# A kernel of four chained attention layers: new places for all steps in the orders of its five engines

## The reference

```
x = L0(ctx, x)    # attention over the context, 4-wide GELU, self attention of the norm, skip
x = L1(x, ctx)    # linear attention with elu, norm
x = L2(x, ctx)    # 16 heads of self attention, 16 heads over ctx, 8 experts (top 2), residuals
x = L3(x, ctx)    # 16 causal heads, norm, 16 heads over ctx, norm, ffn of 512 with relu, norm
```

```
scores = einsum('bhqd,bhkd->bhqk', q, k) / sqrt(dh)
attn   = softmax(scores);  out = einsum('bhqk,bhkd->bhqd', attn, v)
h1 = gelu(einsum('nd,efd->enf', hf, fc1_w) + fc1_b)
eo = einsum('enf,edf->end', h1, fc2_w) + fc2_b
```

## Time and profile before

| | |
|---|---|
| three runs | 2834.36 us median (2832.34 to 2839.7) |
| the profiled execution | 2836.33 us, of which the span from first to last instruction is 2834.1 |
| granted clock of TensorE, mean | 0.913 |
| PE busy | 2400.3 us, 85%, 27712 matmuls |
| PEld | 1672.2 us, 59% |
| DVE | 1536.4 us, 54% |
| ACT | 1521.5 us, 54% |
| POOL | 544.8 us, 19% |
| DMA queue of SP | 79.91 MB, 11.5% of 16 engines' span |

### The profile page before, as it was taken

How to read it: one execution, slowest core, us unless ns; L and a number is a source line. 1 busy time by engine, 2 the same in 40 slices (tenths; PEclk the granted TensorE clock), 3 DMA queues, 4 the chain that set the end, 5 groups by cost and what they waited for, 6 DMA issues and landing times. The chain is left out here.

```text
span 2834.1 us, 69952 instructions
## 1 busy us (share of the span) xinstructions
PE 2400.3 (85%) x27712; PEld 1672.2 (59%) x27712; DVE 1536.4 (54%) x4449; ACT 1521.5 (54%) x2379; POOL 544.8 (19%) x730
## 2 busy tenths in 40 slices
PE   3656989898989989898989889897989989888975
PEld 2434647575666657575666657574756657564643
DVE  3343555656465565656465665656465565634232
ACT  1324545565665555665656655665555565644432
POOL 2111112121212222121212121121212122111111
PEclk9555989999999999999999999999999999998965
DMA  2100010111010110101010101111010111110000
...
DMA packets 103752, 84.21 MB, mean 30 GB/s; under 512 B 15000, under 2 KB 102681, under 8 KB 102937
## 3 DMA queue, kind: packets, MB, share of 16 engines
q1 hardware_dynamic: 103449, 79.91, 11.5%
...
...
## 5 line engine op out<-in xcount | busy, mean ns | idle before, releaser
L984 DVE TENSOR_REDUCE smax<-by_query_banks 128x8 f32<-128x616 f32 (+1 forms) x512 | 515.9, 1008 | 353.6 <-PE by_query_banks L1303 353.1
L770 ACT ACTIVATE probs<-by_key_banks 77x1024 f32<-77x1024 f32 (+1 forms) x512 | 517.8, 1011 | 216.7 <-PE by_key_banks L1325 213.3
L1240 PEld LDWEIGHTS by_key_banks<-moe_w,hid 128*128 128x128 f32 x4096 | 476.0, 192 | 14.1
L1240 PE MATMUL by_key_banks<-moe_w,hid 128*128 128x128 f32 x4096 | 483.7, 275 | 0.0
L752 ACT ACTIVATE hid<-by_query_banks,cols 128x512 f32<-128x512 f32 x512 | 334.9, 686 | 274.0 <-PE by_query_banks L1231 272.0
L1373 PE MATMUL weighed_bank<-probs,values 128*32 128x128 f32 x8192 | 365.3, 301 | 2.2 <-ACT probs L770 1.6
L1303 PE MATMUL by_query_banks<-k_int,q_int 32*128 32x128 f16 (+1 forms) x4096 | 199.9, 220 | 166.5 <-DVE smax L984 87.3
L1303 PEld LDWEIGHTS by_query_banks<-k_int,q_int 32*128 32x128 f16 x4096 | 121.7, 99 | 334.0 <-issue 220.1
L1373 PEld LDWEIGHTS weighed_bank<-probs,values 128*32 128x32 f32 x8192 | 211.0, 117 | 95.3 <-issue 45.7
L1325 PE MATMUL by_key_banks<-q_int,k_int 32*128 32x128 f16 x4096 | 223.2, 233 | 8.1 <-ACT probs L770 5.3
L765 ACT ACTIVATE m_sb<-turned_bank 16x128 f16<-16x128 f32 x256 | 67.7, 264 | 298.1 <-PE turned_bank L1355 298.1
(11 more groups left out here) (232 smaller groups left out, 3878.5 us busy)
## 6 DMA issues: line engine op xcount, KB each, us to landing
q_int<-q_nat SPq DMA_DIRECT2D x256, 128.0 KB, 2.7
k_int<-k_nat SPq DMA_DIRECT2D x128, 128.0 KB, 2.7
k_int<-k_nat SPq DMA_DIRECT2D x128, 77.0 KB, 2.3
...
q_int<-m_sb SPq DMA_DIRECT2D x256, 4.0 KB
...
```

Of the source, the lines that this page charges most:

```text
L770: act.activation(probs[h % 2][0:nk], by_key[0:nk], ACT.Exp, scale=DH ** -0.5)\
L984: dve.tensor_reduce(smax[h // 2 % 2][:, pair, :], scores, AX.X, ALU.max, negate=True)\
L1240: last = pe.matmul(B[e % 2][:, seq_tok(b)], hidden[e % 2][:, c, seq_tok(b)], moe_w2[:, e, c, :], start=(c == 0), stop=(c == CHUNKS - 1))
```

## The change

The five strings of TURNS are replaced by others of the same length with the same number of each letter. The length is 232 letters, one for each step of HEAVY, LIGHT, LAYERS and INPUTS. Nothing else differs: the instructions of each step, the streams' own orders, the buffers and the semaphores stay. The first line for PE:

```diff
 TURNS = {
-    "PE": "iiiiiihxlhhxxxllhlhllhhllhxlhlhllhhxhhlhhllxhhhlhlhhllhhlllhhhhxxxhhhhhhxhxhxhhhhhhxhhhhhhhhhhxh"
+    "PE": "ihxlhhxhlxlhllhllhlhxxlhlhlhhhllhxhlhlxhhlhihlhhlhlhlhhlhihxxhhlihhhhxxhxhhhxhhihhxhhhhhhhhhhhxh"
...
 }
```

More of the change, by code:

```diff
@@ L127 @@
-    "SP": "iiiiiillllllxxxxxhhhhhhhhhhhhhhhhhhhhhhhhhhhhhhhhhhhhllllllllllllllllxxxxxxhhhxhhhhhhhhhhhxxxhhh"
-          "hhhhhhhhhhhhhhhhhhhhhhhhhhhhhxxxxxxxxxxxxxxxxxxxhhhhhhhhhhhhhhhhhhhhhhhhhhhhhhhhhhhhhhhhhhhhhhhh"
-          "hhhhhhhhhhhhhhhhhhhhhhhhhhhhhhhxxxxxxxxx",
+    "PE": "ihxlhhxhlxlhllhllhlhxxlhlhlhhhllhxhlhlxhhlhihlhhlhlhlhhlhihxxhhlihhhhxxhxhhhxhhihhxhhhhhhhhhhhxh"
+          "hhhhhihxhhhhhhhhhxhhhhhhhxhhhhhhhhhhxhhhhxhhxhhhhhxhhhhhhhhxhhhhhhhhxhhhhhhhhxxhhhhxhxxhhhhhhhhh"
+          "xhhhhhhxhhhhxxxxhxhxhhhhxxhhhhxhhxxhhhxh",
@@ new lines @@
+    "ACT": "hxhhlhllhlhxlllhixhilllxhlhhxhhxhihlllhlhhxhlhhlhlhihhhhhxxllhxihhhhhlhxxhhhhhxihhxhhhhhhhlhhhhh"
+          "xhhhhhhxhhhhhhhhhhhhxhhhhhxhhhhhhhhhhhxxxxhhhhhhhhhhhhhhhhhhhhhhxhhhhhxhhhxhhxhxhhhhhhhhhxhxhhhh"
+          "hhxhhhhhxhxhhxxxhxhxhxxhhhhhhhxhhxhhxhhx",
+    "DVE": "lhxlxxhlhlllhxhlhhllllhhxlhihhhlxhhhlhlhlllxhhllhhllhhhhxxhhxhhhihhhhhhxhhhxhxhhhhhhhhhhhhhhhxhx"
+          "hhhxhhhhhhhhhhxhhhxhhhhhhhhhhhhhhhhhhxxhhxhhhhhhhhxhhhhhhhhhhxhhhxhhhhhhxhhhxhxhhhxhhhhxhhhhhhhx"
+          "hhhhhhhxhhxhxxxhxxhxihxhihhhhihhxxxhxhih",
@@ new lines @@
+    "POOL": "xhlllhxhhhhhhlllhhhhhhhhhhlllhhlhhhhhhhhhhhhhhhhhhhhhhhhhhhhhhhhhhhhhhhhhhhhhhhhhhhhhhhhhhhhhhhh"
+          "hhhhhhhhhhhhhhhhhhhhhhhhhhhhhhhhhhhhhhhhhhhhhhhxlhhlhllxhlllllhlhxhhllxxxxxxxxxxhxxxxxhxxxhhxhxh"
+          "hixhxxihhihhhxhxihxxxxxixhxhhxxhxxhxxihh",
+    "SP": "hhhihxxlhhxihlhlhhhihlhhlihihlhixhhhhxhhhhhlxhlhhlllhhhhhxhhxxhlhxhhhxhhxhhhhhhlhhlllxhhlxhhhhhh"
+          "xxhhhhhhlhhxhxhhhhhhllhhhxxhhxxhhhhhhlxhhhhhhhhhhhxhhxxhlhhxhhhhhhhhhhhhhhxhxxhxhhhhhxhhhhhxhxhh"
+          "hhhhhhhhhhhhhhhhhxhxhhxhxxhhxhhxhxhhhxhh",
```

## The result

The changed kernel takes 2946.4 us (median of 4 runs, 2934.2 to 2961.5), the kernel before 2833.4 us (2826.2 to 2839.7) beside it: a ratio of 1.0405, 95% interval 1.0378 to 1.0432. That is 113 us slower; the forecast was 100.

The account below looks back on a forecast made before the run. It took PE, busy 85% of the span in a tight chain with reductions and exponentials, as the bound. Terms summed to 7.3 us a pass, 95 over thirteen passes, plus 5 outside: 2934 us, 3.5% slower; 80% range 2874 to 2980.

Parts of the forecast that it names:

- A: SELF2's seven copies, issued later, hold ACT at proj2, and DVE's proj2 half delays a reduction; 3.2 us a pass.
- B: SELF3's copies: max3_2's copy goes behind query2's seven, so PE waits for it in score0_1; 1.7 us a pass.
- C: Norm n32 on DVE now precedes back0_0, so max2_1 on PE waits for o_norm; 0.8 us a pass, router included.
- D: End of the pass: PE reaches caq_turn before hat is complete; 1.6 us of waiting, 0.45 us a pass kept.
- E: Experts: in3_1 waits for gelus, x1_elu stands later, l1_hat delays out4_1 and out6_0; 0.75 us a pass.
- F: The gain: query0 on PE fills the wait between score1_3 and score1_4, -0.1 us a pass; other listed moves are free.
- G: The clock: waits of 3 us can bring one more stretch at 1.2 GHz; 0.5 us a pass.
- second rival: New PE waits among the heads lower the clock more: 3.8 us instead of 0.5, 10.6 a pass, 2980 us; 14%.
- Faster: query0 in PE's gap at the heads' start keeps the clock up, giving back up to 3.8 us a pass; 2821 us; 5%.

Follow-up runs that it names:

- x1: The kernel before with only two SyncE copy steps moved, max1_1 ahead of proj0 and max1_3 ahead of query0; 2884.9 us.
- x2: The kernel before with only two SyncE copy steps moved, proj2 ahead of max3_1 and query2 ahead of max3_2; 2873.5 us.
- x5: x4 with the end-of-pass order of TensorE and ScalarE (caq_turn and the steps around it) as in the kernel before; 2845.8 us.
- x6: x4 with VectorE's n32_norm put ahead of score2_3 again, as in the kernel before; 2851.2 us.
- x7: x4 with the returns of x5 and x6 both made in one kernel; 2856.9 us.
- x4: The changed kernel with SyncE's order of the kernel before, all other engines keeping their new orders; 2847.0 us.
- x11: x4 with the experts' order of the kernel before on TensorE, VectorE, ScalarE and GpSimd; 2864.4 us.
- x8: x2 with six matmuls of unused result ahead of TensorE's wait for the late m_sb copy; 2845.2 us.
- x9: The changed kernel with matmuls of unused result in two stalls, eight ahead of score3_4, six ahead of the late m_sb copy's wait; 2929.0 us.

## Why the prediction was right, and where it was not

The time was right (2934 for 2946) and so were the two causes that it put first. But the sum came out by luck in part: of a pass it gave 6.8 us to waits (A to F) and 0.5 to the clock, 7.3 together, and measured were 5.0 us more of idle time and 3.0 us more of slower matmuls, 8.0. The terms were mis-sized both ways, and the errors cancelled.

- **A**, 3.2 us in a pass: ACT waits 2.9 us (I took 2.8), released by the copy named, and PE idles 3.3 us ahead of score3_4. x1 alone costs 3.3 us in a pass, of which 1.0 is slower matmuls. VectorE's part, the 0.4, was not run by itself.
- **B**, 1.7 us: PE waits 2.4 us. x2 costs 2.4 us in a pass, half of it idle time (1.2) and half slower matmuls (1.2). PE's matmul named as waiting, by_key, was wrong: the row is L1303, issued behind the same wait.
- **C** and **D**, 0.8 and 0.45: the waits came, with 1.14 and 1.39 us, and were worth nothing (x5, x6, x7). The step that failed is the one from a wait of PE to the end of the pass. I had discounted D by most of its length for the work that moves behind it, and C by less; neither had earned anything. What the 1.5 us a pass of x4 consist of stays open: undoing C, D or E did not bring them back.
- **E**, 0.75: the waits came (0.2 us on L1240), and the sign was wrong; taking the new order of the experts away costs 17 us (x11).
- **F**: the wait of the value projection for k_nat fell from 12.3 to 2.8 us over the span, unforeseen in that size. What query0 in the gap after score1_3 gave was not run by itself.
- **G**, the clock, 0.5: PE's busy time grew by 3.0 us in a pass with the same instructions, six times the term. This is the term that was mis-sized most.

So the second rival, that the clock falls more often, was largely true as a mechanism (3.0 against its 3.8), and the forecast held only because C, D and E, which undone one by one gave nothing back, had filled its place in the sum with 2.0 us. I gave it 14%, since PE's waits in the middle of the heads left the clock up; those are under 1 us, the new ones mostly 2 to 4. The rows now show low clock from a wait for a copy on, in each pass, which I had noted as not shown. The rival *Faster* found the clock still falling where the heads start, in eleven of the changed kernel's thirteen passes, though for a shorter time in most of them. The Trainium skill, "TensorE: Matmul & The Clock Gate", section on oscillation in real kernels, says that half of the throttled time is lost; here 6.8 us more at the lower level went with 3.0 us more busy time, 44%.

How much of the 113 us the clock is worth in the end stays open: by the medians x8 gives back about two thirds of what a lone stall costs, in the loop of its profiled execution only a fifth, and x9 17 us where two stalls of copies stand in one pass. Nor was it tried which order of the copies would be faster than that of before.
